# A convolution unit of one image at each end, ready one unit earlier, and a bias of the FFN moved to ScalarE in the last 58 chunks

## What is computed

```python
x = x + _L0_conv_ref(_ln_c(x), L0_conv_kernel)     # depthwise 3x3, 'SAME', plus its own input
t = _to_tokens(x)
t = t + _L0_ffn_ref(_ln_t(t), W1, b1, W2, b2)
# _qlinear(x, W, b): y = q_acc(q_mul(x) @ q_mul(W).T); return q_acc(y + q_mul(b))
# _ffn_ref:          h = relu(_qlinear(x, W1, b1)); y = _qlinear(h, W2, b2)
```

## Time and profile before

| | |
|---|---|
| three runs | 3288.11, 3290.78 (median), 3294.91 us |
| the profiled execution's own time | 3289.0 us |
| its span | 3287.3 us |
| busy: DVE, ACT, PE, POOL | 3161.5, 3068.9, 2986.9, 1922.4 us (96, 93, 91, 58% of the span) |
| mean granted clock of PE | 0.979 |
| DMA | 713.58 MB, mean 217 GB/s |

### The profile page before, as it was taken

The page is one execution under the profiler, slowest core; times in us unless marked ns, Lnnn a source line. Parts: engine busy times, 40 slices in busy tenths (PEclk is TensorE's granted clock), DMA queues, the critical chain, the costliest instruction groups (busy, mean ns, idle before and its releaser), DMA issues.

```text
span 3287.3 us, 78227 instructions
## 1 busy us (share of the span) xinstructions
PE 2986.9 (91%) x24902; PEld 2502.7 (76%) x24902; DVE 3161.5 (96%) x11557; ACT 3068.9 (93%) x7282; POOL 1922.4 (58%) x913
## 2 busy tenths in 40 slices
PE   5689999999999999999999999999999999999876
PEld 5577777777877777787777778777777877788644
DVE  8559999999999999999999999999999999999998
ACT  7779999999999999999999999999999999986666
POOL 0005666666666666666666666666666666666676
PEclk9999999999999999999999999999999999999966
DMA  7777777787777777777777778777777877766533
GB/s 222 213 206 218 226 228 226 229 232 224 232 226 229 226 229 232 225 230 228 228 226 229 232 223 231 228 228 224 231 231 225 230 227 229 226 199 179 158 118 102
DMA packets 277434, 713.58 MB, mean 217 GB/s; under 512 B 35001, under 2 KB 35106, under 8 KB 277026
## 3 DMA queue, kind: packets, MB, share of 16 engines
q1 hardware_dynamic: 271394, 694.12, 72.6%
q10 hardware_dynamic: 5632, 14.45, 1.3%
HBM read 539.84 MB, written 168.59 MB: 216 GB/s over the span
## 4 chain that ended last, share of the span: by engine, by line
DVE 52%; ACT 23%; PE 18%; issue 5%; DMA 2%; POOL 1%; DVEq 0%; SPq 0%; POOLq 0%; ACTq 0%
DVE stats L650 16%; DVE xq L687 14%; PE conv_ps L430 11%; ACT images L522 10%; DVE hid L640 9%; ACT hid L502 7%; DVE hid L645 6%; PE hid_ps L393 3%; PE y_ps L408 3%; ACT images L533 2%; DVE images L699 2%; ACT y L510 2%; DVE y L667 2%; DVE rstd L678 1%; DVE xt_ps L674 1%
## 5 line engine op out<-in xcount | busy, mean ns | idle before, releaser
L430 PE MATMUL conv_ps<-images,band_ring 112*112 112x222 f32 (+1 forms) x8928 | 1872.8, 354 | 30.2 <-DMA band_ring<-bands 29.5
L430 PEld LDWEIGHTS conv_ps<-images,band_ring 112*112 112x112 f32 x8928 | 1545.6, 177 | 177.9 <-issue 31.5
L275 POOL TENSOR_TENSOR xf<-xf,y 112x768 f32<-112x768 f32 x448 | 953.0, 2127 | 1101.1 <-DVE y L667 1101.1
L502 ACT ACTIVATE hid<-hid_ps 128x896 f16<-128x896 f32 x1344 | 1234.1, 931 | 89.6 <-PE hid_ps L393 89.6
L270 POOL TENSOR_TENSOR xf<-xf,images 112x768 f32<-112x768 f32 x448 | 982.2, 2192 | 259.7 <-ACT images L533 246.4
L522 ACT ACTIVATE images<-xn,neg_mean,rstd 112x96 f32<-112x96 f32 x2800 | 1088.1, 561 | 15.8 <-DVE neg_mean L682 11.3
L408 PEld LDWEIGHTS y_ps<-w2t,hid 128*128 128x128 f16 x10752 | 584.8, 100 | 365.8 <-ACT hid L502 194.4
L408 PE MATMUL y_ps<-w2t,hid 128*128 128x96 f16 x10752 | 668.3, 210 | 190.1 <-ACT hid L502 159.9
L687 DVE SCALAR_TENSOR_TENSOR xq<-xf,stats,xt_ps 112x96 fp8e5<-112x96 f32 x3584 | 840.5, 310 | 0.0
L393 PE MATMUL hid_ps<-xt,w1t 96*128 96x448 fp8e5 x2688 | 681.0, 363 | 16.9 <-ACT xt L494 16.9
L640 DVE TENSOR_SCALAR hid<-hid,b1q 128x896 f16<-128x896 f16 x1344 | 583.9, 466 | 12.8 <-ACT hid L502 12.3
(11 more groups left out here) (54 smaller groups left out, 763.5 us busy)
## 6 DMA issues: line engine op xcount, KB each, us to landing
band_ring<-bands SPq DMA_DIRECT2D x744, 294.0 KB, 5.1
xf<-in_x SPq DMA_DIRECT2D x462, 336.0 KB, 5.1
out<-xf SPq DMA_DIRECT2D x448, 336.0 KB, 3.9
xn<-in_x SPq DMA_DIRECT2D x434, 336.0 KB, 3.4
bands<-images ACTq DMA_DIRECT2D x16, 882.0 KB, 7.8
xf<-bands SPq DMA_DIRECT2D x24, 294.0 KB, 4.3
xf<-in_L_ffn_W SPq DMA_DIRECT2D x2, 144.0 KB, 2.8
xf<-in_L_conv_kernel SPq DMA_DIRECT2D x3, 3.4 KB
```

Source lines behind the costliest of these rows:

```text
L275: pool.tensor_tensor(res, res, y[:, e % 2], ALU.add).then_inc(summed, CW)
L430: mm = pe.matmul(dst[:, :, lo:hi], band_place(t < CONV_AT + UNIT, n)[:, PAIR * dx + i, :], images[:, m % 2, :, ch, lo + dx - 1:hi + dx - 1 ...
L502: nc.scalar.activation(hid[:, e % 2, TOK * j:TOK * (j + 1)].rearrange("p (u n) -> p u n", u=2), hid_ps[:, k, :, 0:HALF * H], ACT.Identity) ...
```

## The change

1. **Half units at both ends.** `CONV_AT` is 14 steps earlier (-43). The first unit holds image 0 alone and the last one image 31 alone, so there are 17 units; the 15 between hold images 1 and 2, 3 and 4, and so on. In a half unit each matmul has 112 moving columns in place of 224, and `save_conv` copies 224 values in place of 448. The number of matmuls, of saves and of band matrices per unit is the same.
2. **Bands in thirds.** They are built 384 columns a time, 6 builds a step in place of 5, third 2 first. Thirds 0 and 1 are used for the first half unit where they were built (`bands_at`), without a load; third 2 is loaded back. Sends stand at fixed steps (`SEND_AT`). The ring has 3 places from the start, and `xf` lends none.
3. **First 42 chunks one step earlier.** Their moments, root, reciprocal and negated mean (not the normalised columns) run one step sooner (`early`), with x in a ring of four; before, a ring of four held for the first 28.
4. **PE's waits** for `ffn1` stand at `ffn1` itself, for each part of it; `at_last` is gone. Part 1 no longer waits for the cast of part 0.
5. **ScalarE adds the third part's bias** in chunks 390 to 447 (`add_last_bias`); DVE adds two.
6. `statistics_c` no longer waits for ACT's normalised columns, `invert_c` does.

```diff
-        CONV_AT = -UNIT - 1
+        CONV_AT = -UNIT - 1 - CHUNKS
+        UNITS = B // IMGS + 1
+        FIRST_NORMS = UNIT + CHUNKS
+        ACT_BIAS = max(0, TOTAL - LOOP - 2)
+        def unit_images(t):
+            m = (t - CONV_AT) // UNIT
+            return slice(1, IMGS) if m == 0 else slice(0, 1) if m == UNITS - 1 else slice(0, IMGS)
+        def early(t, lag):
+            late, soon = t + lag + LOOP, t + lag + LOOP + 1
+            return [n for n in (late, soon) if 0 <= n < TOTAL and (n == soon) == (n < FIRST_NORMS)]
+        STAGES = [(1, 1), (0, 0), (1, 0)]
+        BUILT = (2, 0, 1)
+        STAGED_AT = {CHUNKS: 2, 2 * CHUNKS: 0, 3 * CHUNKS: 1}
+        SEND_AT = {2: (4, 1), 0: (14, 2), 1: (22, 2)}
-        STEP_SETUPS = 5
+        STEP_SETUPS = 6
+        LOADED_FROM = 2 * TGROUPS
+        def bands_at(n):
+            if n < LOADED_FROM:
+                return band_stage(n // TGROUPS)[:, n % TGROUPS]
+            return band_ring[:, (n - LOADED_FROM) % BAND_RING]
...
+                def ffn1(e, j):
+                    k = (J * e + j) % 2
+                    if j == 0:
+                        wait(pe, xt_copied, e + 1)
+                    wait(pe, hid_cast, J * e + j - 1)
...
-                        mm = pe.matmul(dst[:, :, lo:hi], band_place(t < CONV_AT + UNIT, n)[:, PAIR * dx + i, :],
-                                       images[:, m % 2, :, ch, lo + dx - 1:hi + dx - 1], start=(dx == 1),
+                        mm = pe.matmul(dst[:, imgs, lo:hi], bands_at(n)[:, PAIR * dx + i, :],
+                                       images[:, m % 2, imgs, ch, lo + dx - 1:hi + dx - 1], start=(dx == 1),
...
+                def add_last_bias(e):
+                    j = J - 1
+                    act.wait_ge(hid_cast, J * e + j + 1)
+                    part_j = hid[:, e % 2, TOK * j:TOK * (j + 1)]
+                    nc.scalar.activation(part_j, part_j, ACT.Identity, bias=b1q[:, j:j + 1]).then_inc(act_biased, 1)
...
+                    if ffn_in(t - 2) and t - 2 >= ACT_BIAS:
+                        add_last_bias(t - 2)
                     if ffn_in(t - 1):
                         copy_xt(t - 1)
```

More of the change, by code:

```diff
@@ L141, in metaformer @@
         band_col = [sem("band_col_dve"), sem("band_col_act")]
-        bands_out = [sem(f"bands_out{i}") for i in range(QUARTERS)]
+        bands_out = [sem(f"bands_out{i}") for i in range(THIRDS)]
         xn_in = [sem(f"xn_in{i}") for i in range(FIRST_NORM_RING)]
@@ L212, in band_place @@
[L212 to L224, removed]
@@ L227, in setups, with band_arrival @@
+        def band_arrival(n):
+            return band_in[(n - LOADED_FROM) % BAND_RING], dma_count(n - LOADED_FROM, BAND_RING)
+        def setups(t):
             n = STEP_SETUPS * (t - NORM_AT)
-            return range(n, min(n + STEP_SETUPS, QUARTERS * SETUPS)) if c == t and n >= 0 else range(0)
+            return range(n, min(n + STEP_SETUPS, THIRDS * SETUPS)) if n >= 0 else range(0)
         def run(eng, step):
-            for c in range(NORM_AT - 1, LOOP_AT):
-                step(0, c, c)
@@ L233, in run @@
[L233 to L238, removed]
+            for t in range(NORM_AT - 2, END):
+                step(t)
         with nc.Block() as block:
@@ L333, in step @@
+                def step(t):
+                    for n in early(t, 3):
+                        load_xn(n)
                     if ffn_in(t + 3):
-                        wait(sp, x_out[(c + 3) % FFN_RING], dma_count(r, c + 3 - FFN_RING, FFN_RING))
+                        wait(sp, x_out[(t + 3) % FFN_RING], dma_count(t + 3 - FFN_RING, FFN_RING))
                     if ffn_in(t - 3):
-                        store(r, c - 3)
+                        store(t - 3)
                     if ffn_in(t + 3):
-                        load_xf(r, c + 3)
@@ L574, in step @@
-                    if ffn_in(t - 1):
-                        cast_hid(r, c - 1, 1)
-                    if norm_in(t + 2):
-                        root_c(r, c + 2 + LOOP)
-                    if ffn_in(t - 1):
-                        cast_hid(r, c - 1, 2)
+                    for third, (at, every) in SEND_AT.items():
+                        k, off = divmod(t - NORM_AT - at, every)
+                        if 0 <= k < SENDS and off == 0:
+                            send(third, k)
+                    if ffn_in(t - 1):
+                        cast_hid(t - 1, 2)
```

409 lines of the change are left out of this document (192 added, 217 removed).

## The result

The changed kernel takes 3342.15 us (median; 3337.75 to 3343.41), the kernel before in the same comparison 3289.45. The ratio is 1.0156, 95% interval 1.0138 to 1.0173: slower by 51 us, where 3254, faster by 35, was forecast. The time lies above the range, and close to none of the mechanisms that were priced.

A forecast was written before the change was run, and what follows sets the result against it. DVE, busy 2652.22 of 2653.20 us, was taken to bound the full stretch, which stays; 22 us at the start and 15 at the end took 3289.0 to 3252, and 1.8 for the median gave 3254 us, range 3236 to 3286.

The forecast's parts named there:

- a loop ends later: Last 56 steps: the path from rounding through ACT's bias back to rounding sets the step, about 5.5 us.
- half clock: Last 14 steps: PE's halves of y and parts of ffn1 take twice as long, so a step is about 5.9 us.
- The bias: End of the kernel: ACT's addition of the third part's bias costs 0.95 us.
- The end: Last chunks: 2.7 us from the first 14 steps, 11.6 from 28 half steps, 0.6 from the last 14; 15 gained.
- Half matmuls at 0.10: Half units: each matmul with half the columns takes 0.10 us, against 0.19 for a full one.
- rival B: Half units: a half matmul costs as much as a full one, so 3288 us, within the tolerance; chance 0.13.
- Full stretch unchanged: Middle of the kernel: DVE's instructions stay the same, so 388 chunks still take 6.84 us each.
- The start: Steps before the FFN: its first reciprocal comes at 220 us in place of 241, a gain of 22 with smoother entry.
- the ring: Four places for x at the start, each held for landing, two steps and 0.8 us; 3.0 us a step taken.
- The lower bound of 8 us for the start: Steps before the FFN: the smallest gain, with both data stretches at 3.8 us a step.
- Rival A: Start of the kernel is starved of data: start gains 8 us, end 9, so 3274 us; chance 0.17.
- Rival C: Half units: PE falls to half clock, a step at the end takes 7.5 us, so 3316 us; chance 0.08.

The follow-up runs named there:

- s5: The kernel before with PE's waits for ffn1 placed at ffn1 itself, each part for its own cast, and nothing else: 3280.21 us, ratio 0.9956.
- e1: The changed kernel with DVE adding all three parts of the bias everywhere again: 3267.87 us, ratio 0.9929.
- e4: The changed kernel with POOL adding only one of eight columns of the FFN's result in the last 59 chunks: 3269.97 us in one run.

## Why the prediction was wrong

The forecast had the span 37 us shorter; it is 52.8 longer. Of these 90 us, 74 lie between marks 391 and 447 (+59 in place of -15), 4 behind them, and 12 ahead of them (-10 in place of -22).

- **"DVE loses a third of 1.77: 5.84 - 0.59 = 5.25. But a loop ends later", 4.10 + 0.37 + 0.95 + 0.1 = 5.5.** This step failed. The loop is there and is what ends last, with ACT's bias ahead of the rounding as I had said; but I carried the rounding's 0.85 into a place where POOL runs. The measured loop is 7.27 in the step above, where the granted clock is 0.50. For half clock the prediction had 5.9, and there too the trace agrees (ACT waits 0.21 for `ffn1`, the casts start 0.3 later); what was missing is 1.21 for the rounding and 0.1 at ACT's bias. The trace of before could have told. A bias on DVE has a mean of 466 ns on its page but 637 in its last stretch, and three take 1.77, where a pair takes 0.81 in the step above, so three should take 1.2. In that step the first of the three takes 1.05 and the others 0.44 each: it already ran into POOL's second addition, which ends 0.25 us before it does. I took the 1.77 as it stood. And I held DVE's order of work against ACT's and PE's only: POOL's place between b2 and the rounding, which the wait opened, was in none of my terms.
- **The bias, 0.95 from start to start, 1.05 long: right.** 0.93 from its start to the next instruction's, and 1.03 to 1.06 long.
- **The end, -15 us.** Without the bias it is 337.9 against 350.4 us from mark 391 to 447: -12.5. Its parts: first 14 steps 6.48 (6.5 said), the 28 half steps 5.93 and 5.90 (5.85), last 14 steps 5.83 (5.8); only, the half steps get there without ACT's help. That is partly luck: DVE is busy there without a gap and sets these steps, where the forecast had the loop through ACT. With the bias, +59. The first 14 steps, which I gave no bias at all, carry it too: it begins at chunk 390.
- **Half matmuls at 0.10, not 0.16 or 0.19: right.** In the changed kernel, 6 of them take 0.59 us from start to the next group's:

```profile
3100.87 0.75 PE L425 MATMUL conv_ps<-images,band_ring 112*112 112x112 f32 x6
3101.46 0.68 PE L403 MATMUL y_ps<-w2t,hid 128*128 128x96 f16 x12
```

  So rival B is out. The 81 ns that the Trainium skill gives in "TensorE: Matmul & The Clock Gate" under "Back-to-back issue gap" for a matmul of 128 columns with its own weights doesn't hold for these: 98 ns for an instruction that I had taken as two such passes.
- **Full stretch unchanged: right,** 6.832, some 3 us less in all; in s5, which has only PE's new waits, it is 6.829, so this is theirs.
- **The start, 220 us: mechanism right, size wrong.** I wrote the ring as 4 s = L + 2 s + 0.8 and chose 3.0 a step; the change needs 94.5 us from the last build to the half unit's end, not 89, 53.1 for the steps with builds, not 47.7 (DVE's moments wait 3.1 for x there), and 70.1 for the first full unit up to the FFN, not 67.5. Without the early step these are 85.7, 48.7 and 66.8. Of the 22 us for the start 9 came; without the early step, 24. The lower bound of 8 us for the start was also added up wrongly: 3.8 a step in both data stretches is 16 us more, which leaves 6. I had taken part 3 of the change as a help to ACT's loop and didn't price the same line with one step in place of two.
- **Rival A** named this starvation: its start of 8 us is e1's 7.9, and it gave 3274 for a kernel whose bias costs nothing, where e1 took 3268. Its sign was a wait of over 15 us in the first 150; the moments of the changed kernel wait 14.0 for x there, so the sign was set a little high. **Rival C**, the slower side, gave 3316 by a low clock. The clock was 0.94 from mark 405 to mark 433 and 0.58 after, and 0.99 and 0.63 in e1 with steps under 6: it isn't what made the change slower. In the stretch with the first half unit, which C had slow too, it was 0.93. The sign that C held was the right one, for a mechanism that wasn't in it, and 0.09 was too little for what a new wait on the busiest engine can open.

## What to carry to other kernels

Before work is moved off a busy engine, list what a neighbour that can exclude it does in the gap that the new wait leaves: here 0.44 us of waiting cost 1.2 us more, since it turned over which of DVE and POOL came first. An instruction's duration is read at its own place and with the same work beside it, and groups of equal instructions with different durations in the trace before are the warning. A pipeline's step taken earlier is not free while its input holds a place in a short ring: count the steps from landing to the last reader.

## What I had not expected of the hardware

- A rounding of 2688 16-bit values on DVE takes 0.84 to 0.91 us in the changed kernel when it starts first, 0.86 in e4 when first by 0.03 us, and 1.52 or 2.06 when POOL's addition started 0.83 or 0.30 us before it. POOL's addition of 768 values takes 1.64 when first and 2.12 behind a rounding, the other one 2.19 and 2.80 to 2.89.
- Moments and subtract-and-multiply on DVE beside the same POOL additions kept their 1.10 and 1.87 us.
- A bias of 896 float16 values on ACT takes 1.03 us where a cast of as many from PSUM takes 0.91.
